# Attention scores in three overlapping key tiles from rotated queries, one PSUM bank per group's sums, down products in the next batch's iteration, and a new call order, in a decoder layer on one core

## What is computed

```python
scores = matmul(Qw, Kw.T) * scale          # 16 heads of 32, one shared key and value head
wout = matmul(_swat(scores), Vw)           # sigmoid scores, divided by their sum
# windows of 128 tokens that start every 64 (i = 0, 64, 128, 192); neighbours are blended
x = x + out @ wo.T

# second part: a recurrence over time per channel (k from the normalised x, v from ctx)
y = (A * p + E * vt) / (A * q + E)

# third part: FFN of 2048, ternary weights, activations rounded to 8 bits
h = silu(bit_linear(x, w_gate)) * bit_linear(x, w_up)
h = rms_norm(h, ln_weight)
x = x + bit_linear(h, w_down)
```

## Time and profile before

| | us |
|---|---|
| median of 3 runs | 1200.78 |
| lowest, highest | 1197.72, 1201.48 |
| the profiled execution | 1201.09 |
| its span, first to last instruction | 1199.8 |

### The profile page before, as it was taken

How to read it: one execution, slowest core, us unless ns; L and a number is a source line. 1 busy time by engine, 2 the same in 40 slices (tenths; PEclk the granted TensorE clock), 3 DMA queues, 4 the chain that set the end, 5 groups by cost and what they waited for, 6 DMA issues and landing times.

```text
span 1199.8 us, 25113 instructions
## 1 busy us (share of the span) xinstructions
PE 934.9 (78%) x9924; PEld 592.0 (49%) x9924; DVE 818.6 (68%) x1599; ACT 747.1 (62%) x1225; POOL 445.1 (37%) x495
## 2 busy tenths in 40 slices
PE   6866755769797878888897979797978888887565
PEld 3345443455555555554554555555545545555222
DVE  4745665966776767777676766676767677776664
ACT  0137472594949494958667685949494948577543
POOL 2100212443434344444444444434343444344433
PEclk9996796999999998999999999999999999999978
DMA  9984420122222222121223223232222221213022
GB/s 303 381 302 166 124 89 1 46 55 72 63 72 62 49 87 47 53 68 48 76 53 80 55 63 72 63 72 64 71 63 47 77 58 53 64 28 81 18 62 61
DMA packets 145093, 101.09 MB, mean 84 GB/s; under 512 B 93552, under 2 KB 128592, under 8 KB 143824
## 3 DMA queue, kind: packets, MB, share of 16 engines
q1 hardware_dynamic: 140112, 94.92, 27.5%
q10 hardware_dynamic: 4208, 1.95, 0.6%
q0 software_dynamic: 656, 2.63, 0.6%
HBM read 67.49 MB, written 11.01 MB: 65 GB/s over the span
## 4 chain that ended last, share of the span: by engine, by line
PE 38%; ACT 30%; issue 10%; DVE 9%; POOL 8%; DMA 4%; SPq 1%; ACTq 0%; DVEq 0%; POOLq 0%
PE bank L574 12%; ACT arena L706 8%; PE bank L471 7%; PE bank L531 7%; PE bank L489 5%; POOL sums L1298 4%; PE bank L584 3%; ACT L706 3%; ACT work L742 2%; ACT sums L713 2%; ACT L713 2%; ACT junk L758 2%; ACT L729 1%; ACT L758 1%; ACT sums L718 1%
## 5 line engine op out<-in xcount | busy, mean ns | idle before, releaser
L1315 POOL TENSOR_TENSOR work<-junk,lnw 128x512 f32<-128x512 f32 x128 | 175.8, 1382 | 272.4 <-DVE junk L1122 262.0
L574 PE MATMUL bank<-w_up_gate,qT 128*128 128x512 bf16 x1024 | 231.6, 380 | 7.4 <-DMA qT<-q_tok 3.6
L574 PEld LDWEIGHTS bank<-w_up_gate,qT 128*128 128x128 bf16 x1024 | 97.1, 98 | 126.9 <-issue 6.3
L489 PE MATMUL bank<-wide,k_pair 32*128 32x192 f32 x2048 | 106.7, 347 | 66.5 <-ACT arena L706 53.8
L503 PE MATMUL bank<-arena,one_win 128*32 128x128 f32 (+1 forms) x2560 | 89.4, 293 | 81.1 <-ACT sums L713 40.7
L584 PE MATMUL bank<-w_down,work 128*128 128x512 bf16 x512 | 123.9, 393 | 26.7 <-DMA work<-work 26.7
L531 PE MATMUL bank<-wo_sb,wide 128*128 128x512 f32 x256 | 118.6, 618 | 29.3 <-DVE wide L1016 29.3
L489 PEld LDWEIGHTS bank<-wide,k_pair 32*128 32x128 f32 x2048 | 87.1, 194 | 93.3 <-ACT arena L706 74.0
L1122 DVE TENSOR_TENSOR junk<-bank,junk 128x512 f32<-128x512 f32 x128 | 86.4, 687 | 60.6 <-ACT junk L758 24.1
L503 PEld LDWEIGHTS bank<-arena,one_win 128*32 128x32 f32 x2560 | 79.7, 124 | 93.5 <-issue 47.6
L471 PE MATMUL bank<-wide,wq_sb 128*128 128x256 f32 x512 | 118.4, 386 | 5.1 <-DVE rows L1023 5.1
(11 more groups left out here) (144 smaller groups left out, 1659.6 us busy)
## 6 DMA issues: line engine op xcount, KB each, us to landing
rows<-in_x SPq DMA_DIRECT2D x24, 512.0 KB, 4.7
sums<-in_xT SPq DMA_DIRECT2D x16, 512.0 KB, 9.0
wide<-in_xT SPq DMA_DIRECT2D x16, 512.0 KB, 4.3
kv_b<-k_raw SPq DMA_DIRECT2D x64, 128.0 KB, 2.8
ctx_T<-in_ctxT SPq DMA_DIRECT2D x16, 512.0 KB, 5.4
out<-rows SPq DMA_DIRECT2D x32, 256.0 KB, 2.6
wide<-in_x SPq DMA_DIRECT2D x8, 512.0 KB, 9.0
work<-in_wgT SPq DMA_DIRECT2D x4, 1024.0 KB, 10.7
```

Source lines behind the costliest of these rows:

```text
L489: last = te.matmul(bank[j][:, kt * QW:(kt + 1) * QW], k_pair[head, n, kt * P:(kt + 1) * P], q[head, c, kt * BLK:kt * BLK + QW], start=n == ...
L574: last = te.matmul(bank[4 + k % 4][:, :], qT[:, c, t * P:(t + 1) * P], w_up_gate[:, m, c, cols], start=c == 0, stop=c == NC - 1)
L1315: ge.tensor_tensor(hid_w[:, t, cols], hid[:, n % 2, :], lnw[:, cols], op=ALU.mult).then_inc(z_set.sem, 1)
```

## The change

1. **Scores.** The queries are fully rotated before the scores. `rope` is as before, but then 16 copies per batch, issued by SyncE (`turn_queries`), write `q_sin` with exchanged halves into `q_swap` (the buffer of the transposed input `xT`), and VectorE adds it to `q_cos` (`rotate`, two adds). The keys are kept once (`k_win`); their exchanged copy goes, in the first stage too. There are three key tiles of 128 that start every 64 tokens, each against the 128 queries of its own window: 3 x 4 = 12 products of 128 columns for four heads.
2. **Sums.** Each window's tile gives its own 128 columns, and the last window's second half 64 more: 4 products per head for 5. The sums of group c are in bank c; `nums(b, c)` writes the same bank once `logs` has read it. Banks 4 to 7 are the FFN's alone.
3. **Down products** of batch g = i - 3 stand amid the gate and up products of batch f = i - 2, one iteration later than before.
4. **Order.** The calls of all five engines are in a new order.

The core of the difference (the lists of calls are shown behind it in excerpts):

```diff
+        def turn_queries(b, k):
+            sy.wait_ge(roped.sem, roped.at(b, 2 * k + 1))
+            sy.wait_ge(q_made.sem, q_made.at(b))
+            for j in range(QUAD):
+                lo, mid, hi = j * HD, j * HD + HD // 2, (j + 1) * HD
+                for to, src in ((slice(lo, mid), slice(mid, hi)), (slice(mid, hi), slice(lo, mid))):
+                    sy.dma_start(q_swap[to, 2 * k:2 * k + 2, :], q_sin[src, 2 * k:2 * k + 2, :]).then_inc(
+                        q_turned[k].sem, 16)
...
         def scores(b, c):
...
-            for kt in range(NT):
-                for n, q in enumerate((q_cos, q_sin)):
-                    for j in range(QUAD):
-                        head = slice(j * HD, (j + 1) * HD)
-                        last = te.matmul(bank[j][:, kt * QW:(kt + 1) * QW], k_pair[head, n, kt * P:(kt + 1) * P],
-                                         q[head, c, kt * BLK:kt * BLK + QW], start=n == 0, stop=n == 1,
-                                         skip_group_check=True)
+            if c % 2 == 0:
+                te.wait_ge(rotated.sem, rotated.at(b, c // 2))
+            for n in range(NW):
+                window = slice(n * BLK, n * BLK + P)
+                for j in range(QUAD):
+                    head = slice(j * HD, (j + 1) * HD)
+                    last = te.matmul(bank[j][:, n * P:(n + 1) * P], k_win[head, window], q_cos[head, c, window],
+                                     start=True, stop=True, skip_group_check=True)
...
+            for n in range(NW):
                 for j in range(QUAD):
+                    te.matmul(bank[k][j * HD:(j + 1) * HD, n * P:(n + 1) * P], by(n), prob[:, n, QUAD * c + j, :],
+                              start=n == 0, stop=True, skip_group_check=True)
+            for j in range(QUAD):
+                last = te.matmul(bank[k][j * HD:(j + 1) * HD, NW * P:OUTS], by(LAST), prob[:, NW - 1, QUAD * c + j, BLK:],
+                                 start=False, stop=True, skip_group_check=True)
...
         def nums(b, c):
             te.wait_ge(v_set.sem, v_set.at(b))
+            te.wait_ge(logged.sem, logged.at(b, c))
+            four_heads(b, c, c, lambda n: v_win[:, n, :]).then_inc(num_made.sem, 1)
...
         def down(f, t, k):
             if k == 0:
                 used_by = hid_set if t else silu_set
-                te.wait_ge(used_by.sem, used_by.at(f, 7))
+                te.wait_ge(used_by.sem, used_by.at(f + 1, 3) if f + 1 < B else used_by.at(f, 7))
...
+        def rotate(b, k):
+            ve.wait_ge(q_turned[k].sem, q_turned[k].at(b))
+            half = slice(2 * k, 2 * k + 2)
+            ve.tensor_tensor(q_cos[:, half, :], q_cos[:, half, :], q_swap[:, half, :], op=ALU.add).then_inc(
+                rotated.sem, 1)
```

568 lines of the change are left out of this document (292 added, 276 removed).

## The result

| | before | after |
|---|---|---|
| time, median (range), us | 1199.8 (1197.7 to 1201.5) | 1262.4 (1261.0 to 1264.9) |
| ratio, 95% interval | | 1.0525 (1.050 to 1.055) |
| profiled span, us | 1199.8 | 1261.0 |
| output products of batch 2 start | 270.4 | 273.9 |
| one period (13 between batches 2 and 15) | 63.9 | 67.5 |

Slower by 5.2% (5.0 to 5.5). The forecast, 1206, had the side right, but as a close call (5 us slower, where 62 were measured); the time lies above its range of 1174 to 1232. The span is 56.1 over the 1204.9 of the sum: 9.9 in the start, 13 x 2.7 = 35.3 in the periods, 10.9 in the end.

What follows compares the result with a forecast made beforehand. No engine was full; a loop of waits through the query copies, VectorE, TensorE and ScalarE was taken to bound the kernel. Start 264 + 13 periods of 64.8 + end 98.5 = 1204.9 span, so 1206; range 1174 to 1232.

Steps and rivals of the forecast that it cites:

- Step 1: VectorE's earlier work and the residual's first half free its bank 8.7 us after the output products start; query products start then.
- step 2: Residual, norm and scales on VectorE, then ScalarE's work and the queries' rotary products, which end at 20.3.
- Step 3: SyncE issues 8 copies, a transpose, 8 copies: 3.7 + 1.3 + 3.7 = 8.7; halves land at 26.1 and 31.1.
- Step 4: VectorE behind the second add: rounding, four scans, values, then the hidden product that frees the up products' bank, ending at 37.5.
- Step 5: Up products, two late score stages and their sigmoids, to 43.7 at full clock; half clock behind TensorE's idle adds 1.9.
- rival at full clock: TensorE stays at full clock in step 5: period 62.9, time 1181, chance 0.30.
- Step 6: ScalarE's five table loads, twelve logs and inverses and a silu take 13.7, covering the previous batch's down products.
- Step 7: GpSimd's last weighing 1.17, VectorE's two products 0.7, recurrence transposes 1.9, gate and up products 1.7: to 62.9 at full clock.
- third rival: Score stages go by the number of products, 1.2 each: period 65.4, time 1214, chance 0.12.
- second rival: The queries' second half lands some 2.4 later, its copies waiting for a transpose's data: period 67.2, time 1237, chance 0.13.
- Start: Time until batch 2's output products, from changes in batches 0 to 2: 264 for 270.4, by estimate within 6.
- End: From batch 15's output products on: 98.5, between 95 and 106, the second-last batch's down products fitting into the last batch's waits.

Runs made afterwards that it cites:

- Run 8: Changed kernel with SyncE's transpose of hidden rows issued behind the second group of copies, not between the two groups: 1237.1 us, ratio 1.032.
- run 10: Run 9's order on VectorE, but GpSimd issues the second half's 8 copies beside SyncE's first 8: 1162.0 us, ratio 0.969.
- run 4: Changed kernel with the four gate products of the second half's first group made four times over, in TensorE's idle: 1242.2 us, ratio 1.036.
- run 7: Changed kernel with the four gate products of the second half's first group made seven times over, in TensorE's idle: 1229.1 us, ratio 1.025.
- run 5: Changed kernel without the rotation: no copies that swap query halves, VectorE adds the unswapped sine products, both adds kept: 1109.3 us, ratio 0.925.
- run 12: Changed kernel with seven of eight of the second-last batch's down products left out in each of four groups: 1258.2 us, ratio 1.050.
- run 11: Changed kernel with 8 copies of 64 KB, scans ahead of both adds, first down products between the first two score stages: 1175.3 us, ratio 0.978.
- run 2: Changed kernel with two hidden products, four scans, values and a rounding moved ahead of VectorE's second add: 1172.1 us, ratio 0.979.
- run 9: Run 2 and run 8 together on the changed kernel, with the second add ahead of the rounding of hidden rows: 1161.6 us, ratio 0.968.
- run 1: Changed kernel with the third and fourth hidden product moved ahead of VectorE's add for the queries' second half: 1187.8 us, ratio 0.993.

## Why the prediction was wrong

Its loop was the right one, and so was the wait that it named in place of the old ones; the term that failed first is the copies' issue, and smaller ones followed. In the period from 615.59 (68.2 us; the mean of 13 is 67.5: one copy of the second group takes 1.27 here, so that the group takes 5.64, and 5.08 or less in the periods behind it), against the working of 64.8:

- *Step 1, query products at 8.7, and step 2, the first half's rotary products by 20.3*: 8.7 and 20.2. Right.
- *Step 3, copies.* This failed. It took 0.47 a copy from the loads of the keys; the copies took 0.63, and the second group 5.64 for 8. That is 3.2 more for 16. Landing gave some back: by the page's median it was 2.0, where 2.6 was taken from a load of another shape. The second add stood at 33.8 for 31.1: **2.7 short** (33.1 to 34.7 in the 13 periods, 33.6 on average). Run 8 shows that such a term goes into the period in full, with clock on top. The Trainium skill, DMA: Bandwidth & Descriptors, section Anatomy of one DMA, has about 2.0 fixed, and gives it for transfers that GpSimd issues; those of run 10 landed in 2.1, SyncE's of 32 KB here in 2.0. The sum by it, 1199, was further off all the same, since not the landing but the issue had been mis-sized. The trace of before had a nearer price in another row: each of SyncE's stores of a table of the keys held it for 0.59, as a copy does (the copies follow each other 0.04 apart):

```profile
26.48 0.59 SPq L266 DMA_DIRECT2D k_raw<-arena  x1
```

- *Step 4, the third hidden product at 37.5*: 39.7. The work behind the second add took 5.9 for 6.4; so 2.2 of the 2.7 stayed.
- *Step 5, 6.2 and 1.9 for the half clock, to 45.6*: 48.2, another 0.4. The 1.9 is what runs 4 and 7 measured, 1.7 and 2.2. The rival at full clock (0.30) had the size right, but its condition did not hold: the idle was 5.54, longer than the 4.58 of the row against it, and the third score stage ran at half clock in all 13 periods.
- *Step 6, 13.7 on ScalarE*: 14.5. Of the 0.8, 0.59 is a wait for the third group's sums at half clock, which the sum left out.
- *Step 7, 5.5*: 5.5, by luck in its parts. Eight transposes stand there and took 1.1, where 1.9 was put for sixteen; VectorE took 1.55 for 0.7, since a step of the recurrence (L1091, 0.68) stands ahead of its two products.
- *Score stages, 1.0 each*: 0.95 at full clock, 1.67 at half. Between 0.8 and 1.2, nearer to the columns; the third rival's 1.2 did not come.

Together 2.2 + 0.4 + 0.8 = 3.4, which is 68.2 - 64.8. Thirteen mean periods make 35 of the 56 us that the span is over the sum.

*The second rival, a later second half (0.13, 1237)* was the right mechanism from another cause. It had the copies wait for the transpose's data; run 8 shows that the transpose costs its issue, and what made the half late is that a copy's issue is dearer.

*Start, 264 by estimate within 6*: 273.9. The terms that the prediction lists (5.7 and 15 less, 7, 5 and 11 more) give 272.7 and not 264, so most of the miss is a sum that does not follow from its terms. By batch they came to 2.6 less for 5.7, 4.2 less for 3, and 10.2 more for 11. The copies stand there too, since run 5 has 249.9. In batch 2 the rounding of the last quarter of the down weights stands behind the second add (236.79), and GpSimd's first weighing of hidden rows, at 243.67, waits for it. The prediction put 11 of the 15 us of rounding on the path and did not ask what it would be queued behind.

*End, 98.5, at most 106*: 109.4. The step that failed is "the second-last batch's down products fit into its waits". They did not: 6.9 us of them stand between the last batch's gate products. But taking seven of eight out gave back only 4.3 of the 10.9 (run 12). Of the rest, 2.5 is half clock behind an idle of 13.5, which the sum had not counted; what is left was not taken apart.

The range was too narrow for what it rested on. A price per copy, read from loads of another shape and bounded from neither side, stood in it 16 times a period. By the mean of the second add, 33.6, steps 3 and 4 carried 13 x 2.0, some 25 of the 56 us.

## What to carry to other kernels

Price a DMA's issue by its count, and bound it from both sides when the only row is one of another shape: here 0.63 on SyncE for 32 KB as for 64, 0.47 for a load of 96 KB and under 0.4 for a store of 256 KB, and 16 in series on one queue cost 153 us in all. Ahead of any wait for such a transfer, look at what stands behind it on the waiting engine and does not need it: moving two instructions ahead of the wait was worth 75 us, 90 with six more. Products placed in a wait of TensorE also held its clock (runs 7 and 11), so they are judged by the products behind them, too. And one period of a trace may not be the typical one: what was expected of run 7 went by one of the only two slow periods of run 4's 13.

## What was not expected of the hardware

- **The issue of a copy within SBUF**: 0.63 for 32 KB and 0.63 for 64 KB on SyncE, 0.50 for 32 KB on GpSimd, where the loads of keys beside them, of 96 KB, take 0.47 (4 in 1.85 to 1.87). The loads of values right behind them, of 8 and 32 KB, take 0.60 to 0.61. The bytes don't set it. What does was not tried.
- **Four scans took 2.43 or 4.16**, and it is not the call that decides: `scan(w, 0)` took 2.43 and `scan(w, 1)` 4.16 in the changed kernel, the other way round in runs 2, 9 and 10. The slow four lie each time beside GpSimd's weighing of two pieces of hidden rows, which itself takes 2.88 there:

```profile
655.33 2.88 POOL L1352 TENSOR_TENSOR work<-junk,lnw 128x512 f32<-128x512 f32 x2 [16.32 <-DVE junk L1147]
```

In run 1 the weighing ran from 610.92 to 613.41, while VectorE waited for the second add. It took 2.49, and both fours were fast:

```profile
618.57 2.43 DVE L1069 TENSOR_TENSOR_SCAN sums<-wkv_s,sums 128x256 f32<-128x256 f32 x4
...
622.15 2.44 DVE L1069 TENSOR_TENSOR_SCAN sums<-wkv_s,sums 128x256 f32<-128x256 f32 x4
```

The Trainium skill, GPSIMD Engine Reference, section 1. Specifications, names an interface to SBUF that GpSimd shares with VectorE's instructions of two SBUF inputs, and the scans have two. The rows agree: in one period of each run, the scans beside the weighing took 4.14 to 4.17 and all others 2.42 to 2.44. That the two slow each other is shown by this; that it is the shared interface is the page's account, which no run tried. It costs 1.7 a period where the order lets the two meet, and nothing where it does not, as in run 1.
- **Products that compute nothing paid**: 24 gate products made over again in each period, 5.2 us at full clock, in an idle of TensorE took 2.2 off it (run 7).
